# Last unit of a long convolution: another order of products, gathers, row statistics and weight conversions

## What is computed

```python
# attention part, X is (4, 2048, 256)
xp = (einsum('btd,de->bte', X, Wp) + bp).reshape(B, T, 4, D)
f = (pos @ Wf + bf).reshape(T, 3, D)
y = xp[:, :, 0, :]
for i in range(3):
    conv = causal_convolution(y, f[:, i])      # written with rfft/irfft, length 2T
    y = conv * xp[:, :, i + 1, :]
x = layernorm(X + y)
# FFN part, hidden size 768, weights int32 / 127
h = silu(x @ wg.T) * (x @ wu.T)
out = layernorm(x + h @ wd.T)
```

## Time and profile before

| what | value |
| --- | --- |
| median of 3 runs | 763.1 us (762.76 to 763.51) |
| profiled execution, its own time | 763.1 us |
| its span, first to last instruction | 761.3 us |
| TensorE busy | 730.4 us, 96% |
| VectorE busy | 554.2 us, 73% |
| ScalarE busy | 490.0 us, 64% |
| GpSimd busy | 420.9 us, 55% |
| mean granted TensorE clock | 0.995 of 2.4 GHz |

### The profile page before, as it was taken

The page is one execution under the profiler, slowest core; times in us unless marked ns, Lnnn a source line. Parts: engine busy times, 40 slices in busy tenths (PEclk is TensorE's granted clock), DMA queues, the critical chain, the costliest instruction groups (busy, mean ns, idle before and its releaser), DMA issues.

```text
span 761.3 us, 16049 instructions
## 1 busy us (share of the span) xinstructions
PE 730.4 (96%) x5936; PEld 547.6 (72%) x5936; DVE 554.2 (73%) x1083; ACT 490.0 (64%) x962; POOL 420.9 (55%) x483
## 2 busy tenths in 40 slices
PE   6999999999999999999999999889999999999995
PEld 5878877888788888888888888545665556655663
DVE  5897777777788888888888888775656666565644
ACT  3454544443378888888877665546776776777753
POOL 3445544455244444344434443789788878888653
PEclk9999999999999999999999999999999999999998
DMA  8759757999899998999989997622445435442312
GB/s 292 228 187 321 258 188 258 317 316 320 299 256 258 258 272 233 269 258 260 244 244 259 311 257 236 226 56 56 100 95 113 110 84 109 87 138 56 64 53 79
DMA packets 193676, 152.69 MB, mean 201 GB/s; under 512 B 35776, under 2 KB 177216, under 8 KB 193344
## 3 DMA queue, kind: packets, MB, share of 16 engines
q1 hardware_dynamic: 191744, 146.36, 67.2%
q10 hardware_dynamic: 1856, 5.31, 2.2%
HBM read 109.45 MB, written 34.34 MB: 189 GB/s over the span
## 4 chain that ended last, share of the span: by engine, by line
PE 88%; DMA 4%; DVE 3%; ACT 2%; POOL 1%; issue 1%; SPq 1%; POOLq 0%; DVEq 0%; ACTq 0%
PE bank L398 22%; PE bank L472 21%; PE bank L452 18%; PE bank L493 10%; PE bank L411 7%; PE bank L432 3%; PE bank L433 3%; PE bank L434 3%; DMA toep<-filter_rows 2%; DVE prod L827 1%; DMA wi<-in_WDT 1%; ACT yl L613 1%; PE bank L509 1%; DMA xt<-in_XT 1%; POOL xs L1049 0%
## 5 line engine op out<-in xcount | busy, mean ns | idle before, releaser
L1022 POOL TENSOR_TENSOR y<-y,gate 128x512 f32<-128x512 f32 (+1 forms) x108 | 124.6, 1159 | 171.9 <-DVE y L852 160.0
L398 PE MATMUL bank<-wps,xs 128*128 128x512 f32 x768 | 182.1, 396 | 10.4 <-DVE wps L785 7.0
L452 PE MATMUL bank<-prod,ei 128*128 128x256 f32 x720 | 186.8, 382 | 0.0
L398 PEld LDWEIGHTS bank<-wps,xs 128*128 128x128 f32 x768 | 144.1, 189 | 42.3 <-POOL xs L1049 11.6
L827 DVE TENSOR_TENSOR prod<-bank,wfx 128x512 f32<-128x512 f32 x180 | 124.3, 690 | 43.5 <-PE bank L411 43.5
L1049 POOL TENSOR_TENSOR xs<-xt,xs 128x256 fp32r<-128x256 f32 x128 | 92.8, 742 | 103.4 <-ACT xs L603 103.3
L472 PE MATMUL bank<-xh,wq 128*128 128x512 f16 x384 | 145.6, 379 | 0.3
L472 PE MATMUL bank<-xl,wq 128*128 128x512 f16 x384 | 145.5, 379 | 0.0
L1041 POOL TENSOR_TENSOR hl<-hf,hh 128x512 f16<-128x512 f32 x95 | 110.7, 1168 | 53.0 <-ACT hh L667 53.0
L452 PEld LDWEIGHTS bank<-prod,ei 128*128 128x128 f32 x720 | 123.4, 191 | 11.6
L632 ACT ACTIVATE y<-bank,iscl 128x512 f32<-128x512 f32 x96 | 66.0, 688 | 87.1 <-PE bank L434 86.7
(11 more groups left out here) (81 smaller groups left out, 1220.8 us busy)
## 6 DMA issues: line engine op xcount, KB each, us to landing
toep<-filter_rows SPq DMA_DIRECT2D x43, 1024.0 KB, 8.1
gate<-gates SPq DMA_DIRECT2D x48, 512.0 KB, 4.3
xt<-in_XT SPq DMA_DIRECT2D x31, 512.0 KB, 5.5
gates<-st SPq DMA_DIRECT2D x24, 512.0 KB, 4.1
gates<-toep SPq DMA_DIRECT2D x24, 512.0 KB, 4.1
xr<-in_X SPq DMA_DIRECT2D x16, 512.0 KB, 4.6
out_x<-oo SPq DMA_DIRECT2D x15, 512.0 KB, 3.2
toep<-filter_rows SPq DMA_DIRECT2D x10, 512.0 KB, 6.8
```

Source lines behind the costliest of these rows:

```text
L398: mm = pe.matmul(b_proj[n % PBK][:, :], xs[:, n % XSS, hx, k, :], wps[:, hw, k, p * 512:(p + 1) * 512], start=(k == 0 and q == 0), stop=(k ...
L452: mm = pe.matmul(b_out[m % 2][:, half * W:(half + 1) * W], ei[:, h, e0 * P:(e0 + 1) * P], prod[:, n % 3, h, :], start=(h == 0), stop=(h == 1))
L1022: nc.gpsimd.tensor_tensor(y[:, u % NG, a:a + count, :], y[:, u % NG, a:a + count, :], gate[:, a:a + count, :], ALU.mult).then_inc(gated, 1)
```

## The change

In the last unit only:

- VectorE: at an odd step from 5 on, `gather` comes after `multiply` of that step. The statistics of tiles 0 and 1, before one block of four `bn_stats` and four `bn_aggr` in steps 5 and 10, are now two pairs of `bn_stats` after the `multiply` of steps 4 and 6 (tile 0) and 10 and 12 (tile 1), with the `bn_aggr` after that of steps 8 and 14. `low_first` goes from step 12 to step 13, behind that step's gather.
- GpSimd: `add(1)` goes from step 7 to step 6; `root` for tile 0 from step 6 to step 9, for tile 1 from step 11 to step 15. At an odd step `apply` comes first.
- TensorE: the transposes of tile 0 go from step 10 to step 11. `gate_part(0, 0)` waits for four converted pieces and no longer for six; the first down product waits for six.
- ScalarE: `cast(4)` and `cast(5)` go behind `split_first`; `norm1(0)`, `split_first` and `norm1(1)` with `split_x(1)` are written at steps 9, 11 and 15 (before 8, 10, 13), which changes nothing in their order.

```diff
--- before.py
+++ after.py
@@ -556,7 +556,7 @@
                         if k == 1 and u + 2 < NU:
                             pe.wait_ge(norm_sum, u + 2)
                             norm(u + 2)
-                        if k == 10 and u == NU - 1:
+                        if k == 11 and u == NU - 1:
                             pe.wait_ge(id_in, 16)
                             pe.wait_ge(toep_out, NU * NQ)
                             transposes()
@@ -567,7 +567,7 @@
                         if k == NA - 1 and u == NU - 1:
                             readout(u, NA - 1)
                         if k == 14 and u == NU - 1:
-                            pe.wait_ge(w_cast, 6)
+                            pe.wait_ge(w_cast, 4)
                             pe.wait_ge(norm_sum, NU)
                             gate_part(0, 0)
                         if k == NA - 1 and u == NU - 1:
@@ -586,6 +586,7 @@
                             if k >= 1:
                                 if k == 1:
                                     pe.wait_ge(z_done, NU * NPAIR)
+                                    pe.wait_ge(w_cast, 6)
                                 down(k - 1)
                 down_last(NA - 1)
 
@@ -743,13 +744,15 @@
                         if u == NU - 1:
                             if k == 1:
                                 nc.scalar.activation(warm[:], ones[:, 0:1], ACT.Silu)
-                            if 1 <= k <= 6:
+                            if 1 <= k <= 4:
                                 cast(k - 1)
-                            if k == 8:
+                            if k == 9:
                                 norm1(0, range(NB))
-                            if k == 10:
+                            if k == 11:
                                 split_first()
-                            if k == 13:
+                                cast(4)
+                                cast(5)
+                            if k == 15:
                                 norm1(1, range(NB))
                                 split_x(1)
                 for k in range(NA):
@@ -866,6 +869,9 @@
                     for b in range(NB):
                         last = nc.vector.bn_stats(bst[:, slot, b, :], src[:, b, :])
                     last.then_inc(stats, 1)
+                    row_means(slot, count)
+
+                def row_means(slot, count):
                     dve.wait_ge(stats, count)
                     if count >= 2:
                         dve.wait_ge(rstd, count - 1 if count < 5 or count >= 2 * NA - 2 else count - 2)
@@ -873,6 +879,12 @@
                     for b in range(NB):
                         last = nc.vector.bn_aggr(mv[:, slot, b, :], bst[:, slot, b, :])
                     last.then_inc(mean_ready, 1)
+
+                def row_pair(k, second):
+                    for b in (2, 3) if second else (0, 1):
+                        last = nc.vector.bn_stats(bst[:, 0, b, :], x1[:, k, b, :])
+                    if second:
+                        last.then_inc(stats, 1)
 
                 def stats1(k, count):
                     dve.wait_ge(x1_ready, k + 1)
@@ -962,16 +974,22 @@
                             factors(u + 2)
                         if k <= 1 and u >= 1:
                             gather(u - 1, NPAIR - 2 + k)
-                        if k >= 5 and k % 2 and u < NU:
+                        if k >= 5 and k % 2 and u < NU - 1:
                             gather(u, (k - 5) // 2)
                         if k % 2 == 0 and u + 1 < NU:
                             low(u + 1, k // 2)
                         if u < NU and k < NE:
                             multiply(u, k)
                         if u == NU - 1:
-                            if k in (5, 10):
-                                stats1(k // 5 - 1, k // 5)
-                            if k == 12:
+                            if k >= 5 and k % 2:
+                                gather(u, (k - 5) // 2)
+                            if k in (4, 10):
+                                dve.wait_ge(x1_ready, k // 6 + 1)
+                            if k in (4, 6, 10, 12):
+                                row_pair(k // 10, k in (6, 12))
+                            if k in (8, 14):
+                                row_means(0, k // 6)
+                            if k == 13:
                                 low_first()
                 for k in range(NA):
                     product(k, 0)
@@ -1056,14 +1074,14 @@
                             apply(u, 0)
                         if k >= 5 and k % 2 and u < NU:
                             apply(u, (k - 3) // 2)
-                        if u == NU - 1 and k in (2, 7, 12):
+                        if u == NU - 1 and k in (2, 6, 12):
                             t = k // 5
                             if t == 2:
                                 pool.wait_ge(x1n_ready, NB)
                             pool.wait_ge(gated, u * NGATE + (t + 1) // 2 + 1)
                             add(t)
-                        if u == NU - 1 and k in (6, 11):
-                            root(0, k // 5)
+                        if u == NU - 1 and k in (9, 15):
+                            root(0, k // 7)
                 pool.wait_ge(gated, NU * NGATE)
                 for k in range(NA):
                     low_h(k, 0)
```

## The result

| | before | after |
| --- | --- | --- |
| median, same chip | 762.93 us (762.13 to 763.51, 4 runs) | 769.09 us (768.36 to 770.22, 4 runs) |
| profiled execution, its own time | 763.1 | 768.54 |
| its span | 761.3 | 766.7 |
| mean granted TensorE clock | 0.995 | 0.992 |

The ratio is 1.0091, with a 95% interval from 1.0079 to 1.0102: the kernel after is 0.9% slower. The forecast was 769.5 us.

What follows compares the result with a forecast made beforehand. TensorE was taken to bound the kernel, with its waits in the end of the last unit. From 763.1 us, 0.7 + 3.0 + 1.3 for waits (+5.0) and +1.4 for the clock gave 769.5 us; range 767.4 to 771.3.

Steps and rivals of the forecast that it cites:

- Term 1: Last unit's loop up to `up_part(0, 0)`: the loop's gain and the longer wait before the transposes nearly cancel, +0.7 us.
- Term 2: First tile: TensorE waits before `gate_part(0, 2)` for `silu(0, 0)`, held behind `norm1(1)`, `split_x(1)` and late `root(0, 2)`, +3.0 us.
- Rival C: The second wait, before `gate_part(0, 2)`, is not there: 763.8 us, or 764.5 with one clock fall; chance 0.05.
- Term 3: First tile to the first down product: TensorE's lead is gone, so VectorE's longer chain shows, +1.2 to +1.3 us.
- Term 4: TensorE's clock falls after both new idle times, 0.7 us each, +1.4 us in all, range 0 to 2.9.
- The casts: ScalarE's conversions moved from ahead of `norm1(0)` to behind `split_first`: worth 0, as `root` now ends at 493.0.
- Rival D: GpSimd's queue doesn't decide and tile 0's `x1n` is ready at 491.1: -3.2, 759.9 us, faster; chance 0.04.

Runs made afterwards that it cites:

- e1: Kernel after, with unread products filling both TensorE idle times, before the transposes and before `gate_part(0, 2)`: 767.72 us, ratio 1.0067.
- e10: Kernel after, with unread products filling only the first idle time, before the transposes: 767.50 us, ratio 1.0068.
- e5: Kernel before, with only the conversions of the last two down weights moved behind `split_first` on ScalarE: 760.83 us, ratio 0.9982.
- e2: Kernel after, with `root(0, 1)` directly behind `apply(1)`, ahead of `add(1)`, on GpSimd: 764.01 us, ratio 1.0019.
- e4: Kernel after, with `root(0, 1)` behind `apply(1)`, tile 1's means at step 12 and `root(0, 2)` ahead of `add(2)`: 761.20 us, ratio 0.9988.
- e11: Kernel after, with unread products filling only the second idle time, before `gate_part(0, 2)`: 768.83 us, ratio 1.0085.
- e3: Kernel after, with tile 1's means at step 12 and `root(0, 2)` ahead of `add(2)`, `root(0, 1)` left late: 765.82 us, ratio 1.0046.
- e12: Kernel before, with only the statistics by pairs and the order that comes with them, including later roots and transposes: 767.88 us, ratio 1.0079.
- e9: e4 with `low_h(0, 2)` ahead of `add(3)` on GpSimd: 762.24 us, ratio 1.0001 to the kernel before.
- e8: e7 with `low_h(0, 2)` ahead of `add(3)` on GpSimd: 758.70 us, ratio 0.9959 to the kernel before.
- e7: Kernel before, with the parts placed anew: gather ahead of product, roots ahead of adds, transposes at step 11, conversions behind `split_first`: 759.18 us, ratio 0.9960.
- e6: Kernel before, with only the gather moved behind the `multiply` of its step in the last unit: 762.56 us, ratio 1.0008.

## Why the prediction was right, and where it wasn't

**Places.** With 1.60 added to the times of after, or 0.47 to those of e1 (its `multiply(4)` is at 481.34), in which the clock held:

| | forecast | e1 | after |
| --- | --- | --- | --- |
| `multiply(9)` | 488.8 | 488.96 | 488.95 |
| `root(0, 1)` begins | 491.4 | 491.62 | 491.61 |
| transposes | 495.2 | 495.48 | 495.47 |
| `up_part(0, 0)` | 504.6 | 505.09 | 507.15 |
| `silu(0, 0)` | 509.6 | 509.91 | 511.97 |
| `gate_part(0, 2)` | 510.25 | 510.55 | 512.60 |
| first down product | 524.2 | 524.20 | 526.24 |

**Term 1**, forecast +0.7, is +1.18 (505.09 less 503.91). The mechanism holds; the price of a gather behind `multiply` was set too low, since two steps take 2.90 (485.74 less 482.84 in after) and not 2.81: 0.33 for each, and not 0.24. In e1 the transposes are 0.28 later than forecast and `up_part(0, 0)` 0.49; 0.1 of what comes between is that `gate_part(0, 0)` begins 0.16 after `low_first` and not 0.05.

**Term 2**, forecast +3.0, is +2.87 in e1 (the hold from 507.21 to 510.08, filled with products) and 2.70 as the idle time of after. Right, as was the reason: `silu` directly behind `split_x(1)`, and that behind `root(0, 2)` behind `apply(6)`. Rival C, a second wait that isn't there, falls.

**Term 3**, forecast +1.2 to +1.3, is +0.96 (13.65 from `gate_part(0, 2)` to the first down product in e1; before 12.69). The size of VectorE's chain was taken from the earlier trace rows, 4.38; after, it is 4.07 (511.05 to 515.12), because `low_x(1)` takes 1.22 and not the 1.53 that it took before, when an `apply` ran beside it.

These three make 5.01, forecast 5.0. That the sum fits better than its parts is luck: +0.48, -0.13 and -0.3.

**Term 4**, the clock, forecast +1.4 as two falls at 0.7, range 0 to 2.9, is +2.04 as one. This is the step that failed, in three places. The bound for one fall, "at most half of 2.9", took the length of the fall from the earlier trace rows; here the clock stayed at 0.50 for 6.8 us, and TensorE worked in 5.3 of them. What it lost is worked out from the same instructions in e1: from the start of the transposes to the next state are 1.74 (493.87 to 495.60), in e1 0.90 (495.01 to 495.91), so 0.84 is the transposes, and 1.2 are the states and readouts. The prediction had that 1.2, but left the transposes out, and then took 0.7, the middle of its range, for a part that was hidden. Little was: the state, the product of VectorE and the readout follow each other, so that a slower TensorE lengthens each step. And the second fall didn't come in this execution; where it came (e10), the waits of the first tile hid all but 0.12 of it.

**The sum against the execution.** 763.1 + 7.05 - 1.60 = 768.55, and the execution took 768.54. The 1.60 is the earlier start of the last unit, for which the prediction had no term. The median of after, 769.09, lies 0.4 below the forecast: the waits gave 5.0 as forecast and the clock 0.6 more, while the 763.1 that I started from was high (762.93 in the result, 761.97 to 762.33 in the later rounds). That two errors of opposite sign nearly cancel is luck too.

**The casts** were set at 0, with the reason that `root` had become the later. e5 shows the other half of that sentence: 1.1 to 1.3 us where `root` is early.

**Rival D** said that an early `root(0, 1)` would give -3.2 with all else as it is. e2 shows +1.92 with just that, because the hold of term 2 stays; with both roots early (e4) it is -0.87. The rival priced the loop alone and forgot the first tile: `up_part(0, 0)` is 20.06 after `multiply(4)` in e2 and 20.09 in e4, before 22.10, so the loop gives 2.0, not 3.2 (0.79 of wait is still there before the transposes), and from there to the first down product e4 takes 16.42, before 15.28.

## To carry to other kernels

A step that is split or moved late on one engine has to be followed through the list of the engine that takes it up: here four small instructions of 1.6 us, whose input was ready 3.3 us before their turn came (486.7 against 490.01 in after), set the time of all four engines. Put the short instructions for which others wait ahead of the long ones for which nobody waits yet, and look at what then is late next in the same queue. An idle time of TensorE costs its clock most where thin work that takes turns with another engine follows it, and almost nothing where the next stage waits for others anyhow.

## What the runs showed of the hardware

**The clock's fall is not tied to an idle time of one length, nor is the fall always as long.** Behind the idle time of 4.0 before the transposes it was at 0.50 for 6.8 us in after and e11, and for 3.4 us in e3; behind 3.1 (e12) for 3.4. After 2.7 us before `gate_part(0, 2)` it fell, for 3.4 us, in e2, e10 and e12, and not in the kernel after. That a stretch at 0.50 had ended 9 us before this idle time in after does not explain it: in e12 one had ended 10 us before it, and the clock fell again. It held behind 0.8 (e2, e4), 1.3 (e4) and 1.5 (e9). The Trainium skill ("TensorE: Matmul & The Clock Gate", section "HAM oscillation — how this bites in real kernels") has it that gaps make the next work start slow; the traces agree for the first idle time, where the transposes took 1.94 in place of 1.06, and leave open why the second one was spared in the kernel after.

**The same program, the same place, and two outcomes.** Around 204 us in the first unit, where no run has an edit, the clock fell in five of the profiled executions (before, e4, e5, e8, e12) and held in the other nine. `multiply(4)` came at 480.63 to 481.81 in the five and 480.12 to 481.65 in the nine, so the fall is part of the scatter of the last unit's start and not all of it. All fourteen had the same idle time of 1.37 or 1.38 ahead of it. The unit's first `multiply` begins at 202.25 to 202.98 in the five and at 203.07 to 203.66 in the nine, so what came of the same idle time went with when the work arrived. From the first `multiply` to the sixth the nine take 7.4 us and the five 8.8, so this fall costs 1.4. Of the 1.60 between before and after, 0.82 is there at that sixth `multiply`; the rest comes in the units `u` = 7 and 8, which take 0.8 longer in the execution of before, and why is open.

**VectorE and GpSimd stand in each other's way in one kind of instruction.** `low_x(1)` (VectorE, two tiles read from SBUF) takes 1.22 when no `apply` runs beside it (after), and 1.28, 1.53, 1.75 and 2.17 us beside one (e4, before, e7, e6), so that sometimes the one waits and sometimes the other; one `apply` beside it takes 1.0 us longer in e6 and e7 (1.74 and 1.73 in place of 0.73) and in e4 (2.25 in place of 1.28, from 502.55). `low_h` shows it too: 1.35 beside the end of `low_x(1)` in after, and 1.16 for the next. The products, gathers and statistics of VectorE keep their durations in the same stretch. The Trainium skill ("SBUF — State Buffer", section "🔬 SBUF: two separate sides") says that a VectorE instruction with two SBUF inputs and GpSimd share a pair of ports as an exclusive lock; these durations agree with it. It is most likely why e4 fell short of its sum by 1.2 (the `apply` that takes 1.0 longer stands ahead of the late `add(3)`) and why e6 gave 0.77 back, but no run had the collision alone, so for them it is argued and not shown.
